# A two-layer attention and expert kernel: router parts side by side, the dense expert by tokens, the third mixture's parts stacked, and new places for every piece

## The reference

```python
x = x + L0_xattn(layernorm(x), ctx, ctx, Wq, bq, Wk, bk, Wv, bv, Wo, bo)   # 16 heads of 16
x = x + L0_ffn(layernorm(x), P_w, U1, U2, U3, W1, W2, b2)
x = x + L1_xattn(layernorm(x), ctx, ctx)                                   # no weights
x = x + L1_ffn(layernorm(x), router_w, w_gate, w_up, w_down, ws_gate_up, ws_down)

# L0_ffn: three routers choose 3 of 12 each, softmax over the 3, dense matrices C1, C2, C3
xa = x @ P_w.T;  Ci = top3_softmax(xa @ Ui.T)
h  = gelu(sum_e C1[:, e] * (x @ W1[e].T))
y  = sum_e C2[:, e] * (h @ W2[e].T) + C3 @ b2

# L1_ffn: 64 experts, 8 per token, at most 128 tokens each; and one shared (dense) expert
logits = x @ router_w.T;  top 8 of softmax(logits), renormalised
y = sum over chosen experts of w * (silu(x @ Wg) * (x @ Wu)) @ Wd
  + (silu(x @ ws_g) * (x @ ws_u)) @ ws_down                                # 192 wide
```

## Time and profile before

| | |
|---|---|
| median of 3 runs | 3026.29 us (3019.12 to 3026.99) |
| profiled execution, own time | 3022.97 us |
| its span in the profile | 3021.2 us, mean granted TensorE clock 0.955 |
| TensorE busy, weight loads | 2744.7 us (91%), 2299.0 us (76%) |
| VectorE, ScalarE, GpSimd busy | 2205.8 us (73%), 1039.5 us (34%), 819.3 us (27%) |
| DMA | mean 108 GB/s |

### The profile page before, as it was taken

How to read it: one execution, slowest core, us unless ns; L and a number is a source line. 1 busy time by engine, 2 the same in 40 slices (tenths; PEclk the granted TensorE clock), 3 DMA queues, 4 the chain that set the end, 5 groups by cost and what they waited for, 6 DMA issues and landing times. The chain is left out here.

```text
span 3021.2 us, 61483 instructions
## 1 busy us (share of the span) xinstructions
PE 2744.7 (91%) x23816; PEld 2299.0 (76%) x23816; DVE 2205.8 (73%) x5944; ACT 1039.5 (34%) x1524; POOL 819.3 (27%) x858
## 2 busy tenths in 40 slices
PE   2599999999999999999999999999999999957886
PEld 1378888888888888888888888888888888737775
DVE  2467888878888878888888788888878887743332
ACT  1223333333343333333333333333333433221111
POOL 1000122222222222222222222222222222234334
PEclk6599999999999999999999999999999999968988
DMA  6633344443333333333333333333333332117775
GB/s 187 189 84 103 106 117 121 120 116 109 99 92 101 100 100 94 84 97 99 93 96 96 93 99 90 82 96 99 100 98 88 92 99 51 44 36 213 207 206 135
DMA packets 321184, 327.31 MB, mean 108 GB/s; under 512 B 45406, under 2 KB 302232, under 8 KB 320893
## 3 DMA queue, kind: packets, MB, share of 16 engines
q1 hardware_dynamic: 287100, 304.20, 35.7%
q0 software_dynamic: 33792, 19.17, 3.5%
HBM read 182.18 MB, written 212.37 MB: 131 GB/s over the span
## 5 line engine op out<-in xcount | busy, mean ns | idle before, releaser
L657 ACT ACTIVATE exps<-second 128x1024 f32<-128x1024 f32 x512 | 525.6, 1027 | 780.6 <-PE second L1146 766.6
L552 POOL DMA_INDIRECT expert_slots<-row_mem,sidx x512 | 508.3, 993 | 791.5 <-PE first L1128 547.4
L1226 PE MATMUL mixp<-w_h,r_part_h 128*128 128x256 f32 x3072 | 668.8, 299 | 40.7 <-DVE hid L911 23.8
L826 DVE TENSOR_REDUCE nm<-first 128x4 f32<-128x1024 f32 x508 | 618.4, 1217 | 93.6 <-PE first L1128 93.5
L1226 PE MATMUL mixp<-w_h,r_part_l 128*128 128x256 f32 x3072 | 609.9, 280 | 0.1
L1226 PE MATMUL mixp<-w_l,r_part_h 128*128 128x256 f32 x3072 | 609.4, 279 | 0.0
L1226 PEld LDWEIGHTS mixp<-w_h,r_part_h 128*128 128x128 f32 x3072 | 467.3, 189 | 98.1 <-DVE hid L911 33.0
L1226 PEld LDWEIGHTS mixp<-w_l,r_part_h 128*128 128x128 f32 x3072 | 468.4, 188 | 0.0
L1226 PEld LDWEIGHTS mixp<-w_h,r_part_l 128*128 128x128 f32 x3072 | 468.2, 188 | 0.2 <-issue 0.2
L911 DVE SCALAR_TENSOR_TENSOR x_mem<-mixp,C,x_mem 128x256 f32<-128x256 f32 x768 | 329.7, 477 | 116.8 <-PE mixp L1226 115.1
L911 DVE SCALAR_TENSOR_TENSOR hid<-mixp,C,hid 128x256 f32<-128x256 f32 x704 | 300.7, 474 | 35.4 <-PE mixp L1226 33.4
(11 more groups left out here) (214 smaller groups left out, 3702.1 us busy)
## 6 DMA issues: line engine op xcount, KB each, us to landing
kst<-k_parts SPq DMA_DIRECT2D x256, 192.0 KB
qst<-q_parts SPq DMA_DIRECT2D x256, 192.0 KB
q_parts<-nat_h SPq DMA_DIRECT2D x128, 256.0 KB
k_parts<-ctx_part_h SPq DMA_DIRECT2D x64, 256.0 KB, 2.4
k_parts<-nat_h SPq DMA_DIRECT2D x64, 256.0 KB, 2.4
q_parts<-nat_l SPq DMA_DIRECT2D x64, 256.0 KB
exps<-in_wgu SPq DMA_DIRECT2D x39, 384.0 KB
expert_slots<-row_mem SPq DMA_DIRECT2D x8, 1284.0 KB, 13.6
```

The costliest lines, as they stand in the source:

```text
L552: pool.e.indirect_dma_start(out=slots_dram, out_offset=bass.IndirectOffsetOnAxis(ap=sidx[b % 2][:, t, k:k + 1], axis=0), in_=row[b % 2][:, ...
L657: act.e.activation(exps[:, j % NU, :, :, :].rearrange("p k t s -> p (k t s)"), second[:, :, :].rearrange("p k s -> p (k s)"), ACT.Exp, sca ...
L826: dve.e.tensor_reduce(nm[u % 2][:, :, 2 * j:2 * j + 2].rearrange("p t k -> p k t"), (mixp_mem if in_mixp(b, kind, j) else first)[:, :, :]. ...
L1226: m = pe.e.matmul(mixp[q % 2][:, t * D:(t + 1) * D], src[i][:, dt, t * P:(t + 1) * P], wmix[n][j][:, l, dt, :], start=(k == 0), stop=(k == ...
```

## The change

Three computations are written otherwise, and all places are new.

1. **r_z.** The high and low parts of the router matrix lie side by side in one tile of 72 columns. The high part of the tokens is multiplied with all 72 at once, the low part with the high 36: 8 products instead of 12. VectorE adds the two halves with two reductions where it copied before.
2. **Dense expert.** The second layer's router weights and the dense expert's are one tile of 448 columns. `d_logits` makes logits and gates in one group with tokens on the partitions (256 columns a tile), `d_up` the ups (192 columns). ScalarE's tanh moves into `d_logits`; VectorE multiplies 128 x 384 instead of 96 x 512. The new `d_swap` transposes the result back (four transposes, copied out by ScalarE) for `d_down`. `d_gate` is gone. `misc` is held from `d_logits` until VectorE has multiplied tanh and gate.
3. **b2.** C3's high, high and low part lie side by side in 36 columns (`c3_parts`, two VectorE instructions more behind `r_top`); their transpose has 36 rows, against b2's high, low and high part stacked. One product a tile in the split type takes the place of a plain one.

The set-up follows: one weight load less, other constants from GpSimd. The core of the diff:

```diff
 PLACES = {
-    "o_proj": 44.64, "ln1R": 45.36, "ln2R": 48.51, "r_turn": 48.92, "r_z": 50.24, "r_top": 51.3,
-    "d_logits": 143.42, "d_top": 150.95, "d_pos": 156.45, "d_gate": 149.31, "d_up": 149.37, "d_down": 163.62,
+    "o_proj": 40.678, "ln1R": 42.883, "ln2R": 43.803, "r_turn": 48.724, "r_z": 50.733, "r_top": 52.644,
+    "d_logits": 143.029, "d_top": 153.175, "d_pos": 163.939, "d_up": 144.882, "d_swap": 151.324, "d_down": 166.701,
...
-SCATTER = tuple(158.5 + 2.5 * i for i in range(16))
-LAST = {2: {"d_gate": 174.6, "d_up": 181, "d_down": 196.6}, 1: {"d_gate": 157, "d_up": 157.1, "d_down": 163.62}}
+SCATTER = tuple(177.209 + 2.5 * i for i in range(16))
+LAST = {2: {"d_swap": 178.6, "d_down": 180}, 1: {"d_up": 160, "d_swap": 166, "d_down": 168}}
+LAST_SCATTER = {3: (166, 1.6), 2: (164.2, 1), 1: (164.2, 0.1)}
...
 # VectorE, r_z
-                    dve.e.tensor_copy(zb[:, :, :, 0:L], misc[:, 0:TILES * 64].rearrange("p (t n) -> p t n", t=TILES)[
-                        :, :, 0:3 * L].rearrange("p t (s l) -> p t s l", s=3)).then_inc(v_z, 1)
+                    for t in range(TILES):
+                        z = misc[:, t * P:t * P + 6 * L].rearrange("p (j s l) -> p s l j", j=2, s=3)
+                        dve.e.tensor_reduce(zb[:, t, :, 0:L], z, AX_X, ALU.add).then_inc(v_z, 1)
 # VectorE, end of r_top
+                    c3 = Cw[b % 2][:, :, 2, :]
+                    dve.wait_ge(v_C, b + 1)
+                    dve.wait_ge(t_c3, b)
+                    dve.e.tensor_copy(c3_parts[:, :, 0:2, :], c3.unsqueeze(2).broadcast_to([P, TILES, 2, L])).then_inc(v_c3, 1)
+                    dve.wait_ge(v_c3, 2 * b + 1)
+                    dve.e.tensor_tensor(c3_parts[:, :, 2, :], c3, c3_parts[:, :, 0, :].bitcast(F32), ALU.subtract).then_inc(
+                        v_c3, 1)
...
 # TensorE, r_z
-                        for i, j in TERMS:
-                            for dt in range(DT):
-                                m = pe.e.matmul(misc[:, t * 64:t * 64 + 3 * L], r_parts[i][:, dt, t * P:(t + 1) * P],
-                                                gT[j][:, dt, :], start=(n == 0), stop=(n == 3 * DT - 1))
-                                n += 1
+                        pe.e.matmul(z, r_parts[0][:, 0, at], gT_both[:, 0, :], start=True, stop=False)
+                        for dt in range(DT):
+                            pe.e.matmul(z[:, 0:3 * L], r_parts[1][:, dt, at], gT[0][:, dt, :], start=False, stop=False)
+                        m = pe.e.matmul(z, r_parts[0][:, 1, at], gT_both[:, 1, :], start=False, stop=True)
 # TensorE, d_logits
-                    claim("misc", (v_ld, b + 1))
+                    claim("misc", (v_ld, b + 1), (v_h1, b + 1))
...
-                            m = pe.e.matmul(misc[:, t * NE:(t + 1) * NE], xdT[:, dt, t * P:(t + 1) * P], rT[:, dt, :],
+                            m = pe.e.matmul(misc[:, t * (NE + FH):(t + 1) * (NE + FH)], xdT[:, dt, t * P:(t + 1) * P],
+                                            wsgu[:, dt, 0:NE + FH],
 # TensorE, dense expert
-                elif what in ("d_gate", "d_up"):
...
+                elif what == "d_up":
+                    claim("first", (v_h2, b + 1))
+                    for t in range(TILES):
+                        for dt in range(DT):
+                            m = pe.e.matmul(bank1[0][:, t * FH:(t + 1) * FH], xdT[:, dt, t * P:(t + 1) * P],
+                                            wsgu[:, dt, NE + FH:], start=(dt == 0), stop=(dt == DT - 1))
+                elif what == "d_swap":
+                    claim("misc", (a_sT, b + 1))
+                    pe.wait_ge(v_h2, b + 1)
+                    for f in range(2):
+                        for t in range(TILES):
+                            m = pe.e.transpose(misc[0:FC, f * S + t * P:f * S + (t + 1) * P],
+                                               s_tok[:, t, f * FC:(f + 1) * FC], ident)
```

More of the change, by code:

```diff
@@ L91, in pieces @@
         placed += [(SUBS * b + p, ("mix", b, n, e)) for n in range(2) for e, p in enumerate(MIX[n])]
-        placed += [(SUBS * b + p, ("scatter", b, i)) for i, p in enumerate(SCATTER)]
+        start, step = LAST_SCATTER.get(NB - b, (0, 0))
+        placed += [(SUBS * b + (start + step * i if step else p), ("scatter", b, i)) for i, p in enumerate(SCATTER)]
         for kind in "AC":
@@ L124, in build @@
     KR = 3
-    NE = rT_in.shape[2]
+    NE = wgu_in.shape[0]
     CAP = 128
@@ L257, in build @@
         exT = [t[:, i, :].rearrange("p (a t) -> p a t", a=DT) for t in xhat for i in range(2)]
-        ehid = [sT_a[:, :, i * P:(i + 1) * P] for i in range(2)]
+        ehid = [router_mem[0:FC, 1, :, i * P:(i + 1) * P] for i in range(2)]
         ey = [X[i // 2][:, i % 2, :] for i in range(NY)]
@@ L265, in build @@
         attn_out = ps("attn_out")
+        gates = misc[:, :].rearrange("p (t n) -> p t n", t=TILES)[:, :, NE:NE + FH]
         q_dram = nc.dram_tensor("q_parts", (2 * NB, D, 3, S), F32, kind="Internal").ap()
@@ L579, in scalar_program @@
             act.wait_ge(t_g, 1)
-            act.e.copy(gT[0][:, :, :], misc[:, 0:DT * 64].rearrange("p (t n) -> p t n", t=DT)[:, :, 0:3 * L]).then_inc(a_g, 1)
+            act.e.copy(gT[0], misc[:, 0:DT * 64].rearrange("p (t n) -> p t n", t=DT)[:, :, 0:3 * L]).then_inc(a_g, 1)
             act.wait_ge(v_bo, 1)
@@ L675, in scalar_program @@
                     act.wait_ge(t_b2, b)
-                    act.wait_ge(t_g, 1)
-                    act.e.copy(c3T[:, :], misc[0:L, 0:S]).then_inc(a_c3, 1)
+                    act.e.copy(c3T, misc[0:3 * L, 0:S]).then_inc(a_c3, 1)
                 elif what == "d_turn":
@@ L687, in scalar_program @@
                     act.e.activation(prob[:, :, :], prob[:, :, :], ACT.Exp).then_inc(a_p, 1)
-                elif what == "d_gate":
-                    b, = a
-                    act.wait_ge(t_gate, b + 1)
-                    act.wait_ge(t_dn, b)
-                    act.wait_ge(v_w, CHUNKS)
-                    act.e.activation(sT_a[:, :, :], misc[0:FC, :].rearrange("p (f s) -> p f s", f=2), ACT.Tanh,
-                                     scale=0.5).then_inc(a_th, 1)
+                    act.wait_ge(t_lg, b + 1)
+                    act.wait_ge(t_sw, b)
+                    act.wait_ge(v_w, CHUNKS)
+                    act.e.activation(s_tok, gates, ACT.Tanh, scale=0.5).then_inc(a_th, 1)
+                elif what == "d_swap":
+                    b, = a
+                    act.wait_ge(t_sw, b + 1)
+                    act.e.copy(sT, misc[0:FC, :].rearrange("p (f s) -> p f s", f=2)).then_inc(a_sT, 1)
                 elif what == "e_turn":
@@ L1188, in tensor_program @@
                         out = misc[:, t * D:(t + 1) * D]
-                        pe.e.matmul(out, ones[:, :], b_rows[:, :], start=True, stop=False)
+                        pe.e.matmul(out, ones[:, :].broadcast_to([P, P]), b_rows[:, :], start=True, stop=False)
                         for i, j in TERMS:
@@ L1274, in tensor_program @@
                     m.then_inc(t_pos, 1)
-                elif what in ("d_gate", "d_up"):
+                elif what == "d_up":
                     b, = a
-                    up = what == "d_up"
-                    claim("first" if up else "misc", (v_h2, b + 1) if up else (v_h1, b + 1))
-                    pe.wait_ge(a_dt, b + 1)
-                    for f in range(2):
-                        c0 = up * FH + f * FC
-                        for dt in range(DT):
-                            m = pe.e.matmul((bank1[0] if up else misc)[0:FC, f * S:(f + 1) * S], wsgu[:, dt, c0:c0 + FC],
-                                            xdT[:, dt, :], start=(dt == 0), stop=(dt == DT - 1))
-                    m.then_inc(t_up if up else t_gate, 1)
+                    claim("first", (v_h2, b + 1))
[3 more added lines that the diff above has]
+                                            wsgu[:, dt, NE + FH:], start=(dt == 0), stop=(dt == DT - 1))
+                    m.then_inc(t_up, 1)
+                elif what == "d_swap":
+                    b, = a
+                    claim("misc", (a_sT, b + 1))
+                    pe.wait_ge(v_h2, b + 1)
+                    for f in range(2):
+                        for t in range(TILES):
+                            m = pe.e.transpose(misc[0:FC, f * S + t * P:f * S + (t + 1) * P],
+                                               s_tok[:, t, f * FC:(f + 1) * FC], ident)
+                    m.then_inc(t_sw, 1)
                 elif what == "d_down":
```

119 lines of the change are left out of this document (68 added, 51 removed), and 24 rows, old and new, of the table HALF_PLACES.

## The result

The changed kernel takes 2945.38 us (median of 4 runs, 2944.09 to 2952.68) against 3024.59 us for the kernel before: a ratio of 0.975 (95% interval 0.973 to 0.976). The forecast was 2964 us, the range 2928 to 3010. The profiled execution has a span of 2944.7 us, 76.5 us less than before.

The account below looks back on a forecast made before the run. The prediction took TensorE, idle only 2.9% of the middle, to bound the kernel, with VectorE (82% busy) next. Its terms, -61 + 6 - 7 + 3 = -59 us from 3022.97, gave 2964 us, range 2928 to 3010.

Parts of the forecast that it names:

- TensorE's work: Router logits, third mixture and dense expert: 0.44 + 0.79 + 0.67 = 1.90 us a batch saved, 61 us over 32.
- almost one for one: Work taken off TensorE shortens the middle by nearly as much, since TensorE idles only 2.9% there.
- The Trainium skill's floor: About 25 ns for products of up to 64 columns; the router logits would then save 0.1 us a batch.
- Waits: TensorE's waits behind r_top, with VectorE's longer chain there: +0.2 us a batch, +6 us.
- The bound given (-1.41): Waits in the middle, us a batch, if r_top's new neighbours cover VectorE's chain whole; -45 us in all.
- the rival in which the waits shrink as well: Middle, behind r_top: most of the 1.41 us of wait a batch goes, 2926 us; chance 0.12.
- the one place: VectorE's long chain at r_top, where TensorE was said to run dry regularly: 1.41 us of wait a batch.
- The clock: TensorE's granted clock over the middle, read as 1.00, the higher of its two levels (2.4 GHz).
- Prologue: First mixture weights' load goes ahead of the query stores, starting 6.9 us earlier: -7 us, bounds 0 and -14.
- Tail: Fifteen scatters instead of eight ahead of batch 31's residual, last logits carrying the gates: +3 us, bounds -4 and +15.
- The maxima's way: Rival: second scores wait for row maxima coming back through SyncE's queue; 3092 us at 1 us late each; chance 0.11.
- The one bank: Rival: misc, held from d_logits until VectorE's product, holds TensorE up 1 us a batch: 2996 us; chance 0.11.

Follow-up runs that it names:

- x_places: The kernel before with its old computations in the new places, on chip A: 2977.9 us, 1.2% under before.
- x_code: The kernel before with the three new computations in the old order, on chip A: 3045.2 us, slower than before by 1.0%.
- t_scat: The changed kernel with the last batches' scatters spread, six instead of fifteen ahead of the residual of batch 31: 2917.0 us on chip A, 2942.1 on chip C.
- p_store: The changed kernel with batch 0's query stores ahead of the first mixture weights' load again, on chip B: 0.979 of before, 5.0 us over the control.
- w_vproj: The changed kernel with v_proj moved ahead of the router logits, on chip B: 3027.2 us, 72.6 over the control.
- best: The changed kernel with the last four batches' scatters spread, one out_turn and one first-score group earlier, on chip C: 2962.1 us, 0.980 of before.
- the control: The changed kernel unaltered, run again beside the altered ones: 2954.7 us on chip B (0.977 of before), 2949.5 on chip C (0.976).

## Why the prediction was right, and where it was not

- **TensorE's work**: forecast -1.90 us a batch, measured -1.59 at the high clock, at which its rows were read. r_z -0.37 (0.44), c3 and b2 -0.72 (0.79), dense -0.50 (0.67). Inside the parts errors cancel. The two b2 products take 0.43 us and not 0.27, and c3, costed at nothing, gives 0.10. Logits and gates take 1.65 instead of 1.81, ups 1.49 instead of 1.36, transposes 0.53 instead of 0.60; but d_down, which the sum left out, costs 0.28 more. It does so in x_places too, with the old computations: that is the order's doing. The undo runs gave 12.7 us for r_z and 18.6 for b2, against the 14 and 25 of the terms. And "almost one for one" holds for this order, not for the old one: in x_code the work falls and the time rises.
- **The Trainium skill's floor** ("TensorE: Matmul & The Clock Gate", section "Back-to-back issue gap") would have left r_z 0.1 us. The section gives it for a single product on its own, and says that in a stream each product's spacing is set by its weight load as well; so the prediction took a figure that is not meant for this stream. Here 72 columns take 0.11 us a product, and undoing the part costs 12.7 us on chip C.
- **Waits**: this step failed, in sign. +0.2 us a batch was forecast, idle fell by 0.8, and 0.4 more came from unchanged work between new neighbours, a term the sum did not have. The chain behind r_top did grow by three small instructions of 0.18 to 0.22 us; the new order covers it all the same, as x_places shows (4.7 us of mixture waits with the short chain, 4.6 with the long one in t_scat). Which of the pieces between the first mixture products covers it is not shown. The bound given (-1.41) held the value; I took the end next to the known cost and not the one next to the cover. In truth it was the rival in which the waits shrink as well, to which I gave 0.12. Nor was r_top "the one place" where TensorE ran dry: the transposes of the maxima waited 13.2 us, 37 times, in the row between the two of the earlier trace rows.
- **The clock**: put at nothing, since the window showed 1.00. The low stretches of before, some 0.3 us a batch, are gone, about 9 us of the middle.
- **Prologue**: -7 forecast, -7.7 measured; p_store gave the 6.6 us of the mark back.
- **Tail**: +3 forecast, +28 measured, over the bound of 15 (which its own terms don't give: 3 + 8.9 is 12). The sum had the scatters ahead of the residual and nothing for those ahead of the last layer norm's power; there they cost 6.8 us, and at the residual 1.2 in this run. On chip A the delays at the power and at the two residuals sum to the 14.7 us that the stretch is longer there. What the stretch lost more than that in this run stays open.
- Two errors of opposite sign, 34 us too little gained in the middle and 25 too little lost in the tail, brought the forecast near the time; 8 of the 19 us that it missed by are the last line of the table of stages, which is not the change's. That the time came out nearer than its parts is luck.
- **The maxima's way**: the cover was computed as 5.0 us, it is 5.24; the way is about 5.5. The rival was nearer than its chance of 0.11 says, and w_vproj shows what it can cost: most of 72.6 us for one such place, the fall of the clock with it.
- **The one bank**: no claim of it grew in the changed order as the rival had it, but in the old order (x_code) it and VectorE cost more than the code saves.

## What to carry to other kernels

Where a hand-made order feeds five engines, an edit and the order around it are one change: here the code alone lost 29 us in the places tried, the order alone won 38, and the code in its own order won over 50 more. Before moving a piece, list what it covers: one projection hid a transfer's return with nothing to spare, and the wait that its move opened brought the clock down too. A mean clock of 1.00 over a long window can hide such stretches; look at short ones. And price the run-out separately: small jobs of an idle engine, hidden in the middle, stand ahead of the last chain there.

## What the runs showed of the hardware

*The same program differs by chip, at the same clock.* On chip A t_scat took 2917.0 us, on chip C 2942.1 (before: 3016.4 and 3024.2); its period was 75.33 and 75.84, the granted clock of the middle 1.00 in both. The rows show one place: the copy of the attention's output on ScalarE (681) behind the 16 products that it waits for (1188). The timelines, first of chip A, then of chip C, where this is one of the two longest of 20 batches:

```profile
1108.70 1.06 PE L1188 MATMUL attn_out<-exps,vx 128*17 128x256 f32 x16
...
1109.82 0.59 ACT L681 COPY out_sb<-attn_out 128x512 f32<-128x512 f32 x1 [1.24 <-PE attn_out L1188]
```

```profile
1116.90 1.06 PE L1188 MATMUL attn_out<-exps,vx 128*17 128x256 f32 x16
...
1119.49 0.58 ACT L681 COPY out_sb<-attn_out 128x512 f32<-128x512 f32 x1 [2.64 <-remote]
```

The copy starts 0.06 us after the end of the products' row in the one, 1.53 us in the other, and the copy of the maxima queued behind it makes v_proj wait. On chip C it comes once in each batch, mostly with 0.7 to 0.9 us. In the tail idle times of 3.5 to 9 us of the same kind stand ahead of ScalarE's exponentials and copies; the four runs on chip A have none, and the kernel before has one of 3.9 us. It may be part of what stays open of the tail. TensorE's recorded ends are modelled, so the rows don't show whether its products end later there or its signal is held back; no run tested it.

*A piece's price depends on its neighbours by more than expected*: one out_turn takes 0.59 us between two score groups (best) and 0.41 with a mixture group behind it (the changed kernel), with no wait recorded.

*A wait can bring the clock down*: with a stop of some 2 us in each batch (w_vproj) the granted clock fell to 0.50 in 18 batches of 24, and a batch with such a stretch took 1.5 us more; without the stop, in the control, in none.
